# A two-layer gated cross-attention kernel: the order of its first DMAs and of its plane traffic is rewritten

## The chip, the cores and the metric

The kernel runs on one core of one Trainium2 chip. The metric is the device time of one execution in microseconds (us); lower is better.

## The reference

Two layers of gated cross-attention work on x of 4 x 512 rows of 256 numbers, with a context of the same size. The change touches the first layer's attention and what is prepared ahead of it:

```python
K = heads(ctx @ Wk.T + bk); V = heads(ctx @ Wv.T + bv)      # 16 heads of 16
Q = heads(layernorm(x) @ Wq.T + bq)
scores = Q @ K.T / 4 - 0.1 * abs(t_k - t_q)                  # 512 x 512 per head and batch
x = x + tanh(g_xattn[0]) * (softmax(scores) @ V @ Wo.T + bo)
x = x + tanh(g_ffn[0]) * (relu(layernorm(x) @ Wq1.T + b1) @ Wq2.T + b2)   # weights rounded to -1, 0, 1
# the second layer: the same attention with relu and no bias, then a layer with 4 experts
```

## The kernel before

Five engines each run a program of their own, written out by hand and tied together by semaphores: TensorE (PE), VectorE (DVE), ScalarE (ACT), GpSimd (POOL), and SyncE (SP), which issues most DMAs. An engine runs its program strictly in order, so a wait holds all that stands behind it.

**The prologue** (0 to 71.9 us) makes K, V and Q of the four batches b = 0 to 3. For each batch PE projects the keys (`project(0, "k", b, c)`, two halves c), the values (`values`), turns the normalised rows (`turn_n0`) and projects the queries. ACT and DVE bring each result out of PSUM in two parts, high and low, into `planes`. This buffer has four units: keys of a batch in units 0 and 1, queries in 2 and 3. So ACT may write the keys of batch b + 1 (`unit_out`) only when SP has stored those of batch b to HBM and the store has landed (`planes_kept0_i`). SP's `store_planes` stores planes with four DMAs each, and `load_stacks(g)` brings a group of four heads back with eight DMAs, laid out for the attention as `stack_q` and `stack_k`. There are 16 groups, four to a batch, and a ring of four stacks (`RING`): slots 0 to 3 are filled in the prologue, all of them from the planes of batch 0.

ACT issues the inputs of the batches 1 to 3 (`load_inputs`) and, after batch 2, seven late loads (`load_rest`). POOL splits the context into parts and copies the rows of constants (`constant_rows`, for the time bias) into all eight half-slots of the stacks.

**The attention** of a group needs each query's maximum first. PE multiplies "raws" (`for_maximum`, eight pairs of heads and query tiles to a group), DVE reduces each pair to maxima, POOL splits them in two parts, PE turns them, ACT keeps them (`keep_maximum`), and SP sends them into the stack (`send_maximum(g)`, two DMAs). Only then may PE start the scores of group g: its first score waits for `max_sent0`. Raws run 14 pairs ahead (`AHEAD`). `FIRST_RAWS` says after which step of the prologue the first pairs stand: (0, 2) means two pairs from pair 0. After the prologue's last load of stacks SP does this, in this order:

```python
                planes_left(sp, l, 2 * B * C)
...
                    for s_ in "kvq":
                        sp.dma_start(w_qkv[s_][:], part(a[f"L1_W{s_}"])).then_inc(sem("w_layer1"), 16)
...
                for g in range(G):
                    if g + 1 < G:
                        send_maximum(g + 1)
```

Of the kernel before, what the change touches and what calls it, by code (L numbers as in the profile page):

```python
# [16 lines left out]
P = 128  # L17
# [24 lines left out]
FIRST_RAWS = {(2, "q", 0): (0, 2), (2, "q", 1): (2, 2),  # L42
              (3, "k", 0): (4, 2), (3, "k", 1): (6, 1), (3, "v", 0): (7, 1), (3, "v", 1): (8, 2),
# [80 lines left out]
def gated_blocks_program(nc, a, out):  # L124
    with ExitStack() as ctx:
# [243 lines left out]
        N_KEYS, N_VALUES, N_ROWS, N_IN, N_REST, N_ATT = 4, 3, 2, 2, 7, 4  # L369
# [72 lines left out]

        def rows_in(b):
            return x[:, b * QT:(b + 1) * QT, :], a["x"][b * S:(b + 1) * S, :].rearrange("(t p) d -> p t d", p=P)
# [22 lines left out]
        def _(sp):  # L467
            for signal, moves in (
                (loaded_keys, ((w_qkv["k"][:], part(a["L0_Wk"])), context_in(0), (bias_qk[:, 0, :], a["L0_bq"]),
                               (bias_qk[:, 1, :], a["L0_bk"]))),  # L470
                (loaded_rows, (rows_in(0), (ident[:], a["ident"]))),
                (loaded_values, ((w_qkv["v"][:], part(a["L0_Wv"])), (bias_v[:], a["L0_bv"].partition_broadcast(P)),
                                 (w_qkv["q"][:], part(a["L0_Wq"])))),
            ):
                for dst, src in moves:
                    sp.dma_start(dst, src).then_inc(signal, 16)
# [20 lines left out]
            for l in range(2):  # L497
# [30 lines left out]
                if l == 0:  # L528
                    store_planes("k", 0)
                    store_planes("q", 0)  # L530
                    planes_left(sp, 0, C)
                    load_stacks(0, "k")
                    store_planes("k", 1)
                    planes_left(sp, 0, 2 * C)
                    load_stacks(0, "q")
                    store_planes("q", 1)
                    load_stacks(1, "k")
                    store_planes("k", 2)
                    load_stacks(1, "q")
# [5 lines left out]
                    load_stacks(RING - 1)  # L545
                else:
# [40 lines left out]
                if l == 0:  # L587
                    clear_rows(G)
                    sp.wait_ge(sem("normalised0"), G)
                    sp.dma_start(w1_raw[:], part(a["L0_W1"])).then_inc(sem("w_ffn0"), 16)  # L590
                    sp.dma_start(w2_raw[:], part(a["L0_W2"])).then_inc(sem("w_ffn0"), 16)
# [5 lines left out]
        def _(pe):  # L597
# [7 lines left out]
            def project(l, s_, b, c, src):  # L605
# [12 lines left out]
                else:  # L618
                    weights, rows = weight_parts(l, s_), src(b)
                    for i, (r, w) in enumerate(PRODUCTS):  # L620
# [5 lines left out]
                        if i == 0 and (l, s_, b) == (0, "q", 0):  # L626
                            pe.wait_ge(sem("parts_low"), C + 5)
# [11 lines left out]
            def values(l, v):  # L639
# [3 lines left out]
                if v == 0 and l == 0:  # L643
                    pe.wait_ge(sem("parts_low"), C + 4)
# [153 lines left out]
            def attention(l):  # L798
# [31 lines left out]
                def scores(g, k, t):  # L830

                    if k == 0 and t == 0:
                        pe.wait_ge(sem(f"max_sent{l}_{g % 2}"), 32 * (g // 2 + 1))
# [1322 lines left out]
```

## Time and profile before

| | before |
|---|---|
| three runs | 740.12 us median (739.31 to 741.78) |
| profiled execution | 741.31 us, span 739.5 us |
| PE busy | 691.2 us (93%) |
| DVE busy | 567.0 us (77%) |
| ACT busy | 453.1 us (61%) |
| POOL busy | 368.8 us (50%) |

The span is what the trace shows of the profiled execution; 1.8 us of its own time lie around it. Busy shares are averages over stages with different limits, so the rows further down are of single stretches.

### The profile page before, as it was taken

The page shows a single profiled execution, that of the slowest core. Times are in us where ns is not written, and L with a number is a line of the kernel's source. Part 1 is how long each engine was busy: PE and PEld are TensorE (multiplying, and loading weights), DVE is VectorE, ACT ScalarE, POOL GpSimd, SP SyncE. Part 2 cuts the span into 40 slices and gives each one's busy share as a digit, 9 for nine tenths or more (in the row PEclk, how much of TensorE's full clock was granted, in tenths as well). Part 3 has the DMA queues.
Part 4 walks back from the last instruction along what each step waited for, and adds up shares of the span by engine and source line. Part 5 has one row for each costly group of instructions (what it writes and reads, how often), then busy time and mean ns, then how long its engine had stood idle before and what let it go on. Part 6 is the DMA issues. An engine that isn't in the chain of part 4 may idle for free.

```text
span 739.5 us, 12829 instructions
## 1 busy us (share of the span) xinstructions
PE 691.2 (93%) x4390; PEld 434.9 (59%) x4390; DVE 567.0 (77%) x1037; ACT 453.1 (61%) x972; POOL 368.8 (50%) x442
## 2 busy tenths in 40 slices
PE   7886999999999899999999999999999899999993
PEld 5654444444443588788663444444444688999983
DVE  6786899999993267575888999999997667666673
ACT  3413888888888464856316888888887324333330
POOL 4641566565555433864500022645662756665543
PEclk9998999999999999999999999999999999999998
DMA  5898645555545434003134455432201432211100
GB/s 184 273 252 220 204 148 178 185 152 181 178 168 217 137 97 132 26 1 101 43 104 121 124 156 180 130 97 78 78 2 60 120 127 73 66 38 44 34 9 16
DMA packets 51423, 87.56 MB, mean 118 GB/s; under 512 B 8661, under 2 KB 16855, under 8 KB 51360
## 3 DMA queue, kind: packets, MB, share of 16 engines
q1 hardware_dynamic: 43184, 71.39, 31.1%
q0 software_dynamic: 4640, 11.54, 5.6%
q10 hardware_dynamic: 3536, 3.81, 2.0%
q8 instruction: 36, 0.59, 0.3%
q14 instruction: 27, 0.22, 0.1%
HBM read 44.92 MB, written 41.63 MB: 117 GB/s over the span
## 4 chain that ended last, share of the span: by engine, by line
PE 59%; POOL 10%; issue 9%; DVE 8%; SPq 5%; DMA 5%; ACT 2%; POOLq 0%; another core or an unknown queue 0%; DVEq 0%; ACTq 0%
PE ps_out L856 10%; PE ps_wide L1053 6%; PE ps_out L1076 6%; PE ps_wide L725 6%; PE ps_a L839 6%; SPq L517 3%; PE ps_a L978 3%; PE ps_misc L839 3%; POOL w_lo L1377 3%; PE ps_a L635 2%; PE ps_a L1065 2%; DMA stack_q<-planes_q 2%; PE ps_out L992 2%; PE ps_wide L652 2%; PE ps_misc L992 1%
## 5 line engine op out<-in xcount | busy, mean ns | idle before, releaser
L1688 DVE TENSOR_REDUCE row_max<-ps_wide 128x2 f32<-128x1024 f32 x256 | 301.7, 1220 | 21.1 <-PE ps_wide L725 20.3
L1199 ACT ACTIVATE probs<-ps_a 128x512 f32<-128x512 f32 (+1 forms) x418 | 199.1, 522 | 28.6 <-PE ps_a L839 26.7
L725 PE MATMUL ps_wide<-stack_k,stack_q 48*128 48x512 f32 x512 | 145.1, 470 | 11.6 <-DVE row_max L1688 4.3
L839 PE MATMUL ps_a<-stack_q,stack_k 62*128 62x512 f32 (+3 forms) x418 | 137.3, 391 | 2.1 <-ACT probs L1199 1.5
L856 PE MATMUL ps_out<-probs,vals 128*17 128x512 f32 x1024 | 134.1, 598 | 0.5 <-POOL probs L1455 0.5
L1199 ACT ACTIVATE probs<-ps_misc 128x512 f32<-128x512 f32 (+1 forms) x222 | 114.0, 514 | 16.5 <-PE ps_misc L839 13.8
L1455 POOL TENSOR_TENSOR probs<-probs,fixes_sb 128x512 f32<-128x512 f32 x64 | 82.2, 1284 | 79.1 <-ACT probs L1199 79.1
L839 PEld LDWEIGHTS ps_a<-stack_q,stack_k 62*128 62x128 f32 (+1 forms) x418 | 63.5, 184 | 67.4 <-ACT probs L1199 30.9
L725 PEld LDWEIGHTS ps_wide<-stack_k,stack_q 48*128 48x128 f32 x512 | 68.4, 184 | 47.0 <-DVE row_max L1688 26.2
L839 PE MATMUL ps_misc<-stack_q,stack_k 62*128 62x512 f32 (+3 forms) x222 | 87.8, 396 | 1.3 <-ACT probs L1199 1.2
L839 PEld LDWEIGHTS ps_misc<-stack_q,stack_k 62*128 62x128 f32 (+1 forms) x222 | 40.9, 184 | 39.1 <-ACT probs L1199 30.4
L1341 ACT ACTIVATE hid1T_hi<-ps_a 128x512 fp32r<-128x512 f32 x38 | 20.8, 598 | 49.6 <-PE ps_a L1065 49.6
L1440 POOL TENSOR_SCALAR max_neg<-row_max 128x16 f32<-128x16 f32 x32 | 8.1, 253 | 85.2 <-DVE row_max L1688 85.0
L1332 ACT ACTIVATE hid<-ps_wide 128x512 f32<-128x512 f32 x38 | 22.7, 599 | 37.2 <-PE ps_wide L1055 37.2
L1076 PE MATMUL ps_out<-w_mo_hi,hid1T_hi 128*128 128x256 f32 x152 | 44.3, 292 | 0.2 <-DVE sorted_rows L2042 0.2
L1076 PE MATMUL ps_out<-w_mo_hi,hid1T_lo 128*128 128x256 f32 x152 | 42.7, 281 | 0.0
L1076 PE MATMUL ps_out<-w_mo_lo,hid1T_hi 128*128 128x256 f32 x152 | 42.7, 281 | 0.0
L1522 POOL TENSOR_TENSOR hid_lo<-hid_full,hid_hi 128x512 fp32r<-128x512 f32 x24 | 30.8, 1303 | 20.3 <-ACT hid_hi L1295 20.3
L1358 POOL TENSOR_TENSOR root<-var_eps,minus_half 128x4 f32<-128x4 f32 x16 | 17.6, 1097 | 43.1 <-DVE var_eps L1634 42.9
L856 PEld LDWEIGHTS ps_out<-probs,vals 128*17 128x17 f32 x1024 | 17.5, 95 | 33.1 <-issue 15.7
L1431 POOL TENSOR_TENSOR planes<-full,planes 128x512 fp32r<-128x512 f32 x16 | 21.6, 1361 | 29.5 <-ACT planes L1137 26.1
L1294 ACT ACTIVATE hid_full<-ps_a,b_cols 128x512 f32<-128x512 f32 x32 | 22.1, 692 | 19.3 <-PE ps_a L978 15.7
(288 smaller groups left out, 1413.1 us busy)
## 6 DMA issues: line engine op xcount, KB each, us to landing
rows_sorted<-blank SPq DMA_DIRECT2D x17, 1040.0 KB, 5.0
planes_k<-planes SPq DMA_DIRECT2D x32, 256.0 KB, 3.7
planes_q<-planes SPq DMA_DIRECT2D x32, 256.0 KB, 3.8
stack_k<-planes_k SPq DMA_DIRECT2D x64, 128.0 KB, 2.9
stack_q<-planes_q SPq DMA_DIRECT2D x64, 128.0 KB, 2.8
w_raw<-in_L_W SPq DMA_DIRECT2D x6, 1024.0 KB, 5.3
stack_k<-planes_k SPq DMA_DIRECT2D x64, 64.0 KB, 2.6
stack_q<-planes_q SPq DMA_DIRECT2D x64, 64.0 KB, 2.7
```

What stands on the lines that cost most here:

```text
L517: sp.dma_start(stack[rows, slot(g):slot(g) + 2 * S].bitcast(F32).rearrange("r (c t) -> r c t", t=S), src[:, i]).then_inc(sem(f"stack_loade ...
L725: mm(raw_slot(l, ("pair", g, p))[:, i * S:(i + 1) * S], stack_q[at, slot(g, c) + q * P:slot(g, c) + (q + 1) * P], stack_k[at, slot(g, c):s ...
L839: mm(score_slot(("tile", n))[:, start:end], stack_k[at, slot(g, c) + k * P:slot(g, c) + (k + 1) * P], stack_q[at, slot(g, c) + start:slot( ...
L856: mm(po[32 * j:32 * j + VW, :], vals[:, k, g * HG + j, :], probs[n % PROBS[l]][:, j, :], start=(k == 0), stop=(k == QT - 1)).then_inc(sem( ...
L992: last = mm((po, pm)[t % 2][:, 0:D], hidden0(b, rows, f)[:, q * P:(q + 1) * P], w2_q[:, f, :], start=(f == 0 and h == 0), stop=(f == FC - ...
L1053: mm(bank, sortedT[r][:, n % 2, c, :], w1_flat[w][:, bass.ds(at + (c * FF + half * S), S)], start=(i == 0 and c == 0), stop=False)
L1076: last = mm(po[:, 0:D], hid1T[r][:, n % 2, f, :], w_mo_part(w, f), start=(f == 0 and i == 0), stop=(f == FC - 1 and i == 2))
L1199: do(probs[n % PROBS[l]][:, j, start:end], score_slot(("tile", n * TILES + t))[:, start:end], ACT.Exp, scale=0.25).then_inc(exp_done, 1)
L1332: do(hid1[:, n % 2, half * S:(half + 1) * S], pw[0][:, half * S:(half + 1) * S], ACT.Gelu).then_inc(sem("hid1_ready"), 1)
L1455: v.tensor_tensor(block_, block_, fixes[:, k % 2, :].unsqueeze(1).broadcast_to([P, HG, P]), ALU.mult).then_inc(sem("fixed"), 1)
L1522: v.tensor_tensor(hidden0(b, "lo", f), hid0_full[:, u % 4, :], hidden0(b, "hi", f), ALU.subtract).then_inc(sem("hid0_low"), 1)
L1688: v.tensor_reduce(row_max[:, g % 2, :, p], raw_slot(l, ("pair", g, p))[:].rearrange("p (i k) -> p i k", i=2), AX, ALU.max).then_inc(sem(f" ...
```

## The change

1. SP's nine first loads come in another order, each with a semaphore as its users need it: the key weight, the context, the value weight, the rows, the identity, the query weight, and the three biases last. The high part of the value weight is made by ACT instead of DVE. ACT starts the inputs of batch 1 behind these parts instead of ahead of them.
2. SP waits for all planes of batch 0, loads the whole stack of group 0 and only then stores the planes of batch 1; the stack of group 1 stands whole between the planes of batches 1 and 2.
3. Two pairs of raws move ahead, into the values of batch 2; of the later ones one each stands in the keys and values of batch 3.
4. Of the seven late loads on ACT's queue three stay. The other four (`w_o`, `bias_2`, `b1_cols`, `order`) go to SP's queue, behind the weights of the second layer.
5. POOL copies the constant rows into the half-slots 1 to 3 only. SP copies the half-slots 0 to 3 to 4 to 7 (four DMAs) behind the last load of stacks; PE waits for them ahead of group 2.

```diff
-FIRST_RAWS = {(2, "q", 0): (0, 2), (2, "q", 1): (2, 2),
-              (3, "k", 0): (4, 2), (3, "k", 1): (6, 1), (3, "v", 0): (7, 1), (3, "v", 1): (8, 2),
+FIRST_RAWS = {(2, "v", 0): (0, 1), (2, "v", 1): (1, 1), (2, "q", 0): (2, 2), (2, "q", 1): (4, 2),
+              (3, "k", 0): (6, 1), (3, "k", 1): (7, 1), (3, "v", 0): (8, 1), (3, "v", 1): (9, 1),
               (3, "q", 0): (10, 2), (3, "q", 1): (12, 2)}
...
                     store_planes("k", 0)
                     store_planes("q", 0)
-                    planes_left(sp, 0, C)
-                    load_stacks(0, "k")
+                    planes_left(sp, 0, 2 * C)
+                    load_stacks(0)
                     store_planes("k", 1)
-                    planes_left(sp, 0, 2 * C)
-                    load_stacks(0, "q")
                     store_planes("q", 1)
-                    load_stacks(1, "k")
+                    load_stacks(1)
                     store_planes("k", 2)
-                    load_stacks(1, "q")
                     store_planes("q", 2)
                     load_stacks(RING - 2)
                     store_planes("k", 3)
                     send_maximum(0)
                     store_planes("q", 3)
                     load_stacks(RING - 1)
+                    sp.wait_ge(sem("rows_in0"), 16 * 2 * N_ATT)
+                    sp.wait_ge(loaded_rest, 16 * (N_FIRST + N_REST))
+                    for i in range(2):
+                        for rows in constant_rows(i):
+                            sp.dma_start(rows[:, RING * S:].bitcast(F32), rows[:, 0:RING * S].bitcast(F32)).then_inc(loaded_rest, 16)
...
                     for s_ in "kvq":
-                        sp.dma_start(w_qkv[s_][:], part(a[f"L1_W{s_}"])).then_inc(sem("w_layer1"), 16)
+                        sp.dma_start(w_qkv[s_][:], part(a[f"L1_W{s_}"])).then_inc(loaded_context, 16)
+                    for dst, src in ((w_o[:], part(a["L0_Wo"])), (bias_2[:], a["L0_b2"].partition_broadcast(P)),
+                                     (b1_cols[:], a["L0_b1"]), (order[:], a["order"])):
+                        sp.dma_start(dst, src).then_inc(loaded_context, 16)
...
+            act.wait_ge(loaded_values, 16)
+            do(w_v_hi0[:], w_qkv["v"][:], ACT.Copy).then_inc(sem("parts_high"), 1)
+            load_inputs(1)
+            act.wait_ge(loaded_rest, 16 * N_FIRST)
...
                 for dst, src in (
-                    (w_o[:], part(a["L0_Wo"])), (gates_raw[:], a["gates"].partition_broadcast(P)),
-                    (bias_o[:], a["L0_bo"].partition_broadcast(P)), (bias_2[:], a["L0_b2"].partition_broadcast(P)),
-                    (b1_cols[:], a["L0_b1"]), (fixes[:], a["fixes"]), (order[:], a["order"]),
+                    (gates_raw[:], a["gates"].partition_broadcast(P)), (fixes[:], a["fixes"]),
+                    (bias_o[:], a["L0_bo"].partition_broadcast(P)),
                 ):
...
-                            pool.dma_start(rows[:, S:].rearrange("r (n t) -> r n t", t=S),
-                                           rows[:, 0:S].unsqueeze(1).broadcast_to([n, RING * 2 - 1, S])).then_inc(sem("rows_in0"), 16)
+                            pool.dma_start(rows[:, S:RING * S].rearrange("r (n t) -> r n t", t=S),
+                                           rows[:, 0:S].unsqueeze(1).broadcast_to([n, RING - 1, S])).then_inc(sem("rows_in0"), 16)
```

SP's program between the planes of batch 0 and those of batch 2, in the kernel before (`planes_k` and `planes_q` are the stores, `stack_k` and `stack_q` the loads; x4 and x2 count DMAs):

```order
L506 DMA planes_q<-planes 64x2x512 x4
L517 DMA stack_k<-planes_k 16x2x512 x2
L517 DMA stack_k<-planes_k 32x2x512 x2
L506 DMA planes_k<-planes 64x2x512 x4
L517 DMA stack_q<-planes_q 32x2x512 x2
L517 DMA stack_q<-planes_q 16x2x512 x2
L506 DMA planes_q<-planes 64x2x512 x4
```

The same place in the changed kernel:

```order
L514 DMA planes_q<-planes 64x2x512 x4
L525 DMA stack_q<-planes_q 32x2x512 x2
L525 DMA stack_q<-planes_q 16x2x512 x2
L525 DMA stack_k<-planes_k 16x2x512 x2
L525 DMA stack_k<-planes_k 32x2x512 x2
L514 DMA planes_k<-planes 64x2x512 x4
L514 DMA planes_q<-planes 64x2x512 x4
```

The key planes of batch 1 are stored behind eight loads where they were behind four, and those loads wait for the query planes of batch 0.

SP's program from the last load of stacks to the maxima of group 1 (`max_rows`), in the kernel before:

```order
L517 DMA stack_k<-planes_k 32x2x512 x2
L567 DMA w_k<-in_L_Wk 128x2x256
L567 DMA w_v<-in_L_Wv 128x2x256
L567 DMA w_q<-in_L_Wq 128x2x256
L524 DMA stack_q<-max_rows 2x8x128 x2
```

And in the changed kernel:

```order
L525 DMA stack_k<-planes_k 32x2x512 x2
L555 DMA stack_q<-stack_q 12x2048
L555 DMA stack_k<-stack_k 14x2048
L555 DMA stack_q<-stack_q 12x2048
L555 DMA stack_k<-stack_k 14x2048
L577 DMA w_k<-in_L_Wk 128x2x256
L577 DMA w_v<-in_L_Wv 128x2x256
L577 DMA w_q<-in_L_Wq 128x2x256
L580 DMA w_o<-in_L_Wo 128x2x256
L580 DMA bias<-in_L_b 128x256
L580 DMA b_cols<-in_L_b 128x8
L580 DMA order_sb<-in_order 128x4
L532 DMA stack_q<-max_rows 2x8x128 x2
```

Eight DMAs more stand ahead of the maxima of group 1.

## Rows read from the trace of the kernel before

**Rows 1.** The chain that ended last, 0 to 92 us: start, us, what.

```profile
48.44 12.22 DMA stack_q<-planes_q
...
81.42 2.38 DMA stack_q<-max_rows
...
83.84 0.38 PE ps_a L839
```

**Rows 2.** Windows: stretch, us, busy of PE, PEld, DVE, ACT, POOL, clock, DMA, GB/s.

```profile
41.90:56.80 14.90, 12.40 (x63) 7.93 (x61) 14.59 (x27) 2.08 (x4) 7.13 (x9) 1.00 1.22 209
56.80:60.70 3.90, 0.04 (x1) 0.00 (x0) 0.69 (x1) 1.72 (x3) 3.11 (x5) 0.95 1.11 296
60.70:67.20 6.50, 6.02 (x19) 4.02 (x19) 4.10 (x5) 1.34 (x3) 0.06 (x1) 0.50 0.79 231
67.20:71.90 4.70, 3.40 (x15) 1.74 (x15) 3.77 (x5) 1.47 (x3) 0.00 (x0) 1.00 0.68 194
83.80:94.60 10.80, 10.76 (x71) 4.60 (x71) 9.34 (x9) 9.10 (x22) 7.31 (x9) 1.00 0.53 175
```

**Rows 3.** Timeline of ACT, 22 to 60 us: start, us, instruction, idle before.

```profile
34.86 0.69 ACT L1136 ACTIVATE full<-ps_a,bias_qk 128x512 f32<-128x512 f32 x1 [1.25 <-PE ps_a L635]
...
40.54 0.60 ACT L1162 ACTIVATE x_hi<-ps_misc 128x512 fp32r<-128x512 f32 x1 [0.41 <-PE ps_misc L908]
...
56.10 0.69 ACT L1136 ACTIVATE full<-ps_a,bias_qk 128x512 f32<-128x512 f32 x1 [10.29 <-issue]
```

**Rows 4.** Timeline of SP's DMA issues, 20 to 67 us.

```profile
28.27 3.29 SPq L506 DMA_DIRECT2D planes_k<-planes  x4
31.73 2.92 SPq L517 DMA_DIRECT2D stack_q<-planes_q  x4
34.69 3.90 SPq L506 DMA_DIRECT2D planes_q<-planes  x4
...
44.82 6.55 SPq L517 DMA_DIRECT2D stack_q<-planes_q  x4
51.41 6.00 SPq L506 DMA_DIRECT2D planes_q<-planes  x4
```

**Rows 5.** Issued in 23.9 to 25.2 and 34.6 to 38.6 us: KB each, median us to landing.

```profile
planes_q<-planes SPq DMA_DIRECT2D x1, 256.0 KB, 5.4
...
planes_q<-planes SPq DMA_DIRECT2D x4, 256.0 KB, 6.2
```

**Rows 6.** Timeline of DVE, 5 to 73 us.

```profile
11.06 0.43 DVE L1921 CAST w_v_hi<-w_v 128x512 fp32r<-128x512 f32 x1 [0.40 <-DMA w_q<-in_L_Wq]
...
41.17 0.69 DVE L1908 TENSOR_TENSOR x_lo<-ps_misc,x_hi 128x512 fp32r<-128x512 f32 x1 [0.31 <-ACT x_hi L1162]
...
61.58 2.36 DVE L1688 TENSOR_REDUCE row_max<-ps_wide 128x2 f32<-128x1024 f32 x2 [4.00 <-PE ps_wide L725]
...
68.14 0.75 DVE L1662 SCALAR_TENSOR_TENSOR planes<-ps_a,bias_qk,planes 128x512 fp32r<-128x512 f32 x1 [2.28 <-ACT planes L1137]
```

**Rows 7.** Timeline of SP's DMA issues, 71 to 84 us.

```profile
71.83 1.23 SPq L506 DMA_DIRECT2D planes_q<-planes  x2
73.10 3.01 SPq L517 DMA_DIRECT2D stack_q<-planes_q  x4
76.16 2.85 SPq L517 DMA_DIRECT2D stack_k<-planes_k  x4
79.19 0.43 SPq L567 DMA_DIRECT2D w_k<-in_L_Wk  x1
...
80.69 1.36 SPq L524 DMA_DIRECT2D stack_q<-max_rows  x2
```

**Rows 8.** Timeline of PE, 65 to 86 us.

```profile
71.91 1.02 PE L603 MATMUL ps_out<-vals 128*17 128x512 f32 x2 [0.21 <-DVE planes L1662]
...
82.65 1.05 PE L856 MATMUL ps_out<-probs,vals 128*17 128x512 f32 x8
```

**Rows 9.** POOL's copies of the constant rows, issued in 45.6 to 48.1 us.

```profile
stack_k<-stack_k POOLq DMA_DIRECT2D x2, 196.0 KB, 10.3
stack_q<-stack_q POOLq DMA_DIRECT2D x2, 168.0 KB, 8.9
```

More of the change, by code:

```diff
@@ L368, in gated_blocks_program @@
         loaded_rest = sem("loaded_rest")
[L369 removed]
+        loaded_context, loaded_queries = sem("context0_then_layer1"), sem("queries0_then_ffn0")
+        N_FIRST, N_IN, N_REST, N_ATT = 4, 2, 3, 4
         block = ctx.enter_context(nc.Block())
@@ L467, in _ @@
         def _(sp):
[L468 to L473, printed above, removed]
-            ):
-                for dst, src in moves:
-                    sp.dma_start(dst, src).then_inc(signal, 16)
+            for signal, dst, src in (
+                (loaded_keys, w_qkv["k"][:], part(a["L0_Wk"])),
+                (loaded_context, *context_in(0)),
+                (loaded_values, w_qkv["v"][:], part(a["L0_Wv"])),
+                (loaded_rows, *rows_in(0)),
+                (loaded_rest, ident[:], a["ident"]),
+                (loaded_queries, w_qkv["q"][:], part(a["L0_Wq"])),
+                (loaded_rest, bias_qk[:, 0, :], a["L0_bq"]),
+                (loaded_rest, bias_qk[:, 1, :], a["L0_bk"]),
+                (loaded_rest, bias_v[:], a["L0_bv"].partition_broadcast(P)),
+            ):
+                sp.dma_start(dst, src).then_inc(signal, 16)
             def load_last(n):
@@ L589, in _ @@
                     sp.wait_ge(sem("normalised0"), G)
-                    sp.dma_start(w1_raw[:], part(a["L0_W1"])).then_inc(sem("w_ffn0"), 16)
-                    sp.dma_start(w2_raw[:], part(a["L0_W2"])).then_inc(sem("w_ffn0"), 16)
+                    sp.dma_start(w1_raw[:], part(a["L0_W1"])).then_inc(loaded_queries, 16)
+                    sp.dma_start(w2_raw[:], part(a["L0_W2"])).then_inc(loaded_queries, 16)
             for i in range(LANDING):
@@ L902, in turn_n0 @@
             def turn_n0(b):
+                if b == 0:
+                    pe.wait_ge(loaded_rest, 16 * N_FIRST)
                 pe.wait_ge(sem("normed"), QT * (b + 1))
@@ L1917, in _ @@
                                 ).then_inc(sem("parts_low"), 1)
-            dve.wait_ge(loaded_rows, 16 * N_ROWS)
+            dve.wait_ge(sem("parts_high"), C + 1)
+            weight_low("v")
+            dve.wait_ge(loaded_rows, 16)
             variance(0, 0, x, 1e-5)
-            dve.wait_ge(loaded_values, 16 * N_VALUES)
-            v.tensor_copy(w_v_hi0[:], w_qkv["v"][:]).then_inc(sem("parts_low"), 1)
-            dve.wait_ge(sem("parts_low"), C + 3)
-            weight_low("v")
             normal(0, 0, x)
-            dve.wait_ge(sem("parts_high"), C + 1)
+            dve.wait_ge(sem("parts_high"), C + 2)
             weight_low("q")
+            dve.wait_ge(loaded_rest, 16 * N_FIRST)
             for b in range(B):
```

34 lines of the change are left out of this document (16 added, 18 removed).

## The prediction

> **What bounds the kernel now.** I read the chain that ended last first. Up to 92 us it shows two waits that are no engine's work: the load of group 1's query stack takes 12.22 us, from 48.44 to 60.67, and PE starts behind it [rows 1]; and the maxima of group 1, sent by SP at 81.42, land 2.38 us later, just when PE takes the scores of group 1 at 83.84 [rows 1]. The windows come next. From 83.8 us PE is busy for 10.76 of 10.8 us [rows 2]: in the attention PE is the bound, one group takes about 10.8 us, and time lost there is not won back. In the prologue it is another matter. DVE is full from 41.9 to 56.8 (14.59 of 14.9 us). Then PE stands still for 3.9 us, and behind this wait the granted clock is 0.50 from 60.7 to 67.2, which is 1.2 GHz instead of 2.4 [rows 2]. In these two stretches and up to 71.9 DVE has only 0.69 + 4.10 + 3.77 = 8.56 us of work in 15.1.
>
> The queues say why. ACT stood for 10.29 us in front of the keys of batch 3, with "issue" as the reason, since it was issuing the seven late loads [rows 3], and SP needed 6.55 us for four loads and 6.00 for four stores, which took 2.92 and 3.29 earlier [rows 4]. All of this falls together with POOL's copies of the constant rows, which landed 8.9 and 10.3 us after their issue [rows 9]. So the prologue has something to give. The rest of the argument is what the new order takes.
>
> **The start of the attention.** I call the moment when PE starts it T0; it is 71.9 now [rows 8]. What I need is the new T0.
>
> First loads: DVE waited 0.40 us at 11.06 for the query weight before it could split the value weight [rows 6]. This goes, and the context's parts begin earlier; but ACT now waits for the biases, which are issued last, ahead of its first results. Below, the gain is nothing if the biases land as late as the query weight did (11.0); above, it is 1.2 us, the time by which the value projection could begin earlier. I take 0.6.
>
> Plane traffic: the last query plane of batch 0 was issued at 23.9 and landed 5.4 us later, at 29.3 [rows 5]; with the 0.6 at 28.7. Until then SP now stands still, where it used to load and store. Eight loads at 0.63 to 0.73 us (2.92 for four [rows 4]) take it to about 33.8. The key planes of batch 1, which were issued at 28.27 [rows 4], are now issued from 33.8 to 37.7, in the place and at the price of the four stores at 34.69 (3.90 us [rows 4], landing after 6.2 us [rows 5], because the inputs of batch 3 are on their way then). So the first half lands at about 41.1 (issued 34.9) and the second at about 43.2. ACT may not write the keys of batch 2 before that: its instruction at 34.86 [rows 3] moves to 41.1. Behind it in ACT's program stand the other half and the two copies of the turned rows: 41.1 + 1.3 = 42.4, the second half from 43.2 to 44.5, two copies of 0.60 to 45.7. The second copy ended at 41.1 before [rows 3]. Batch 2 is thus 4.6 us late, and DVE's last low part of it ends at 46.5 instead of 41.9 [rows 6]. If the stores land after 3.9 us or so, this is 2.3 us less.
>
> From there DVE sets the pace. From 41.9 to 71.9 it was busy for 14.59 + 0.69 + 4.10 + 3.77 = 23.2 us [rows 2]. Two of its reductions now stand ahead of this point, at 2.36 us for two [rows 6]: 20.8 remain. The wait of 4.00 us for the stack [rows 6] goes, since group 1's stack is loaded before POOL's copies begin, which are also 3 of 7 parts of what they were. ACT's seven issues become three. The last wait, 2.28 us [rows 6], lay at the half clock; I keep 1.1 of it and 0.6 for small ones. New T0: 46.5 + 20.8 + 1.7 = 69.0, which is **2.9 us earlier**. Bounds: nothing, if PE's own wait in batch 2 (about 3.5 us between the turned rows and the queries) lets the clock fall there too; and 9 us, if batch 2 is not held at all, from 15.1 - 8.56 = 6.5 of idle DVE and 2.4 of moved reductions.
>
> **The maxima of group 1.** They hang on SP's queue, counted from T0, because SP's last stores wait for the same result of DVE as PE does (71.83 against 71.91 [rows 7, 8]). Before: the stores from 71.83, eight loads of stacks, three weights, and the maxima issued at 80.69 [rows 7], landed 2.38 us after the second of them, at 83.8 [rows 1], which is T0 + 11.9. PE was through with what it could do at 83.7 (82.65 + 1.05 [rows 8]), T0 + 11.8: no slack at all. Now eight DMAs stand in between. The four copies of constants, at the 0.63 us and the gap of a stack load: 4 x 0.64 = 2.6 us. The four loads from HBM, at the 0.43 us and gap of a weight (three took from 79.19 to 80.69 [rows 7]): 4 x 0.49 = 2.0. The maxima then land at T0 + 16.5 and PE waits 4.7 us. Behind the waiting score stand all of PE's raws and weighted sums, so DVE and ACT run dry too.
>
> The landing can also be late: the copies of constants and 1.2 MB of weights and biases lie ahead in the same queue. By POOL's rows, 728 KB took about 10 us [rows 9], 416 KB in four copies would take 6 to 8 us from T0 + 7.4, the weights behind them 3 more, and the maxima would land up to 2 us later. Below it is nothing. SP's other transfers were faster than POOL's, so I add 0.5: **5.2 us of wait**. The Trainium skill ("DMA: Bandwidth & Descriptors", section on the anatomy of one DMA) gives a DMA 2.0 us plus its bytes at 436 GB/s. By that, an estimate, a copy of 112 KB is done in 2.3 us, the addition is nothing and the wait 4.7; POOL's rows, with 8.9 and 10.3 us, do not agree with the page.
>
> **The clock.** A PE wait of 3.9 us was followed by 6.5 us at 0.50 [rows 2]. The new wait is longer, so the clock falls again, now in the stretch where PE is the bound. At its end the old wait had barely reached the fall (mean 0.95 [rows 2]); the new one takes 1.2 us or so of the slow stretch into itself. The 5.4 us left at half speed cost **2.7 us**. Bounds: 0 and 3.3.
>
> **What costs nothing.** The four late loads are used only behind the attention, some 170 us later. PE's new wait ahead of group 2 is for copies that landed a group earlier. The split of the value weight on ACT (0.6 us) lies in ACT's idle start; without that cover it would cost its 0.6.
>
> **The sum.** -2.9 + 5.2 + 2.7 = +5.0 us. Against the profiled execution (741.31 us, span 739.5) that is 746.3; its time is 1.2 us above the median of the runs, 740.12, so for the median I say **745.1 us**.
>
> **Rivals.**
> 1. The start wins nothing: the held batch 2 brings a PE wait with the half clock behind it. For: the 3.9 us wait did so. Against: DVE is busy there and hides some of it. +5.2 + 2.7 and 1.5 for slow projections: +9.4, 749.5 us. Chance 0.18.
> 2. The start wins most of DVE's idle time, 6.5 us, because the stores land soon and ACT is hardly held. +1.4, 741.5 us: no difference. For: other stores land in 4 us when no inputs are on their way. Against: the place of the stores at 34.69 [rows 4, 5]. Chance 0.15. That the change does not do what it says, the maxima being as early as before, would end here too; the order of SP's program excludes it.
> 3. Faster: the prologue loses all its waits and the two moved reductions are free. T0 comes 9 us earlier, and the wait for the maxima stays at 4.7 without a fall of the clock. -4.3, 735.8 us. It decides from 7.9 us of gain at T0 with the fall, from 4.7 without it. For: DVE's idle time adds up to it. Against: SP is idle until 28.7 with 34 us of issues to do, and a wait above 3.9 us without a fall was not seen. Chance 0.07.
> My forecast has 0.60, and its own range is 743 to 748. The range reaches to the cases 1 and 2: 741.0 to 750.0; outside lie rival 3 and the edges of 1 and 2, under 2 in 10. A change under 0.3% (2.2 us) can't be told from none here. Slower 0.77 (the forecast without its lowest edge, and rival 1), same 0.15, faster 0.08.
>
> **What would show it.** Right: T0 near 69 in PE's timeline; ACT's first instruction for the keys of batch 2 near 41, released by a store; no load of stacks over 8 us; SP's maxima of group 1 issued 12.7 us or more behind its last plane stores; a PE wait of 4.5 to 6 us ahead of the first scores of group 1, and a window of half clock behind it. Wrong: that wait is missing or short, or T0 is below 64; or a wait for the second copies of constants stands in front of group 2.

## The result and the profile after

| | before | after |
|---|---|---|
| four runs each | 740.32 us median (739.31 to 741.78) | 748.72 us median (747.47 to 750.60) |
| ratio | | 1.011, 95% interval 1.009 to 1.0131 |
| profiled execution | 741.31 us, span 739.5 us | 747.47 us, span 745.7 us |
| PE busy | 691.2 us | 698.0 us |
| start of the attention (T0) | 71.91 | 70.73 |
| first scores of group 1 | 83.84 | 88.98 |
| first scores of group 1, counted from T0 | 11.93 | 18.25 |

The change makes the kernel 1.1% slower (8.4 us, from 740.32 to 748.72). The start comes 1.18 us sooner and the first scores of group 1 come 5.14 us later. By the end of group 1 the distance is 6.2 us, at 400 us it still is, and so is the distance of the two spans: what comes behind group 1 adds nothing on balance.

ACT's timeline of the changed kernel, 0 to 60 us (start, us, instruction, idle before), answers to [rows 3]:

```profile
11.27 0.69 ACT L1151 ACTIVATE full<-ps_a,bias_qk 128x512 f32<-128x512 f32 x1 [3.13 <-DMA bias_v<-in_L_bv]
...
43.30 0.69 ACT L1151 ACTIVATE full<-ps_a,bias_qk 128x512 f32<-128x512 f32 x1 [8.02 <-DMA planes_k<-planes]
...
46.33 0.61 ACT L1177 ACTIVATE x_hi<-ps_misc 128x512 fp32r<-128x512 f32 x1
...
57.41 0.69 ACT L1151 ACTIVATE full<-ps_a,bias_qk 128x512 f32<-128x512 f32 x1 [3.94 <-issue]
```

The second row is the held batch 2. ACT stands for 8.02 us, and the releaser is the store that SP now issues behind eight loads. The last row is the gain of part 4, 3.94 us of issuing instead of 10.29. The first row is new: ACT waits 3.13 us for the biases, and its first result comes at 11.27.

SP's DMA issues, 29 to 88 us, answer to [rows 4, 7]:

```profile
29.75 2.53 SPq L525 DMA_DIRECT2D stack_q<-planes_q  x4
32.33 2.50 SPq L525 DMA_DIRECT2D stack_k<-planes_k  x4
34.87 3.16 SPq L514 DMA_DIRECT2D planes_k<-planes  x4
...
51.46 5.66 SPq L514 DMA_DIRECT2D planes_q<-planes  x4
57.16 3.65 SPq L525 DMA_DIRECT2D stack_q<-planes_q  x4
...
78.31 0.89 SPq L555 DMA_DIRECT2D stack_q<-stack_q  x1
79.25 0.81 SPq L555 DMA_DIRECT2D stack_k<-stack_k  x1
80.10 0.72 SPq L555 DMA_DIRECT2D stack_q<-stack_q  x1
80.86 0.76 SPq L555 DMA_DIRECT2D stack_k<-stack_k  x1
81.80 0.43 SPq L577 DMA_DIRECT2D w_k<-in_L_Wk  x1
82.27 1.26 SPq L577 DMA_DIRECT2D w_v<-in_L_Wv  x1
83.57 0.47 SPq L577 DMA_DIRECT2D w_q<-in_L_Wq  x1
84.09 0.47 SPq L580 DMA_DIRECT2D w_o<-in_L_Wo  x1
...
86.06 1.38 SPq L532 DMA_DIRECT2D stack_q<-max_rows  x2
```

From the first copy to the maxima 7.75 us pass, where the three weights before took 1.50 [rows 7]: 6.25 us for the eight DMAs more. The four copies take 3.49 of them (0.72 to 0.89 each), the four late loads 1.97, and the weights take 2.29 instead of 1.50. The stores of batch 1 (34.87) landed 7.3 us after their issue (median of the four):

```profile
planes_k<-planes SPq DMA_DIRECT2D x4, 256.0 KB, 7.3
```

PE's timeline, 10 to 92 us, answers to [rows 8]:

```profile
15.98 0.63 PE L926 MATMUL ps_out<-ident_sb,rows_all 128*128 128x128 f32 x4 [2.93 <-DVE vals L1680]
...
46.99 1.22 PE L648 MATMUL ps_a<-x_hi,w_q_hi 128*128 128x512 f32 x2 [4.24 <-ACT x_hi L1177]
...
70.73 1.02 PE L616 MATMUL ps_out<-vals 128*17 128x512 f32 x2 [0.21 <-DVE planes L1675]
...
83.51 1.05 PE L871 MATMUL ps_out<-probs,vals 128*17 128x512 f32 x8
88.98 0.58 PE L854 MATMUL ps_a<-stack_q,stack_k 62*128 62x256 f32 x1 [4.41 <-DMA stack_q<-max_rows]
```

And the windows at these places, with the columns of [rows 2]:

```profile
17.10:23.90 6.80, 6.11 (x15) 4.80 (x15) 3.91 (x12) 1.91 (x4) 5.38 (x6) 0.50 0.87 245
44.40:51.20 6.80, 4.21 (x11) 2.52 (x12) 3.78 (x12) 3.09 (x6) 6.26 (x7) 0.50 0.93 293
51.20:70.70 19.50, 16.90 (x83) 10.71 (x83) 18.33 (x27) 5.93 (x11) 6.60 (x10) 1.00 0.85 207
...
84.60:88.80 4.20, 0.00 (x0) 0.00 (x0) 0.48 (x1) 0.00 (x0) 2.87 (x3) 1.00 0.88 249
88.80:92.20 3.40, 3.22 (x17) 1.64 (x17) 1.97 (x2) 2.34 (x5) 0.00 (x0) 0.50 0.42 121
```

The reader is to see three waits of PE (2.93, 4.24 and 4.41 us), each with a stretch at 0.50, that is 1.2 GHz, at its end or shortly behind. Between 51.2 and 70.7 us DVE sets the pace, with 18.33 of 19.5 us. From 84.6 to 88.8 PE and ACT stand still, DVE has 0.48 us and POOL 2.87 us of work: they wait for two small DMAs. A fourth stretch of half clock falls into group 0:

```profile
70.70:84.60 13.90, 13.83 (x59) 5.49 (x59) 11.15 (x10) 9.26 (x21) 4.52 (x7) 0.75 0.72 170
```

The same 59 matmuls took 11.8 us before, from 71.9 to 83.7 [rows 8]; here PE is through at T0 + 13.8. These 2.0 us hide a part of the wait. So the maxima landed 6.3 us later from T0, and only 4.4 of that shows as a wait.

### The profile page after: what moved, and what is told of

It is laid out like the page before. It is cut to its first block, busy times and chain, and to the rows that moved or that the text cites. A ratio compares the mean times of both kernels' runs of the same rounds, so it can differ in the third digit from the quotient of the medians.

```text
span 745.7 us, 12834 instructions
## 1 busy us (share of the span) xinstructions
PE 698.0 (94%) x4390; PEld 438.7 (59%) x4390; DVE 565.7 (76%) x1036; ACT 454.0 (61%) x973; POOL 369.0 (49%) x442
## 4 chain that ended last, share of the span: by engine, by line
PE 60%; POOL 10%; DVE 9%; issue 9%; SPq 5%; DMA 4%; ACT 3%; POOLq 0%; DVEq 0%; ACTq 0%
PE ps_out L871 10%; PE ps_wide L1068 7%; PE ps_out L1091 6%; PE ps_wide L738 6%; PE ps_a L854 6%; PE ps_a L993 3%; PE ps_a L648 3%; PE ps_misc L854 3%; POOL w_lo L1394 3%; SPq L525 3%; PE ps_a L1080 2%; DVE row_max L1701 2%; PE ps_out L1007 2%; PE ps_wide L665 2%; PE ps_misc L1007 1%
## 5 line engine op out<-in xcount | busy, mean ns | idle before, releaser
L1214 ACT ACTIVATE probs<-ps_a 128x512 f32<-128x512 f32 (+1 forms) x418 | 199.2, 522 | 34.6 <-PE ps_a L854 34.1
L738 PE MATMUL ps_wide<-stack_k,stack_q 48*128 48x512 f32 x512 | 147.0, 476 | 5.3 <-DVE row_max L1701 2.0
L1214 ACT ACTIVATE probs<-ps_misc 128x512 f32<-128x512 f32 (+1 forms) x222 | 114.0, 514 | 18.1 <-PE ps_misc L854 15.2
L854 PEld LDWEIGHTS ps_a<-stack_q,stack_k 62*128 62x128 f32 (+1 forms) x418 | 64.3, 188 | 71.9 <-ACT probs L1214 31.3
L854 PE MATMUL ps_misc<-stack_q,stack_k 62*128 62x512 f32 (+3 forms) x222 | 88.8, 400 | 1.3 <-ACT probs L1214 1.2
L1358 ACT ACTIVATE hid1T_hi<-ps_a 128x512 fp32r<-128x512 f32 x38 | 20.8, 598 | 47.8 <-PE ps_a L1080 47.8
```

The lines of the kernel that those rows point to most:

```text
L738: mm(raw_slot(l, ("pair", g, p))[:, i * S:(i + 1) * S], stack_q[at, slot(g, c) + q * P:slot(g, c) + (q + 1) * P], stack_k[at, slot(g, c):s ...
L854: mm(score_slot(("tile", n))[:, start:end], stack_k[at, slot(g, c) + k * P:slot(g, c) + (k + 1) * P], stack_q[at, slot(g, c) + start:slot( ...
L1214: do(probs[n % PROBS[l]][:, j, start:end], score_slot(("tile", n * TILES + t))[:, start:end], ACT.Exp, scale=0.25).then_inc(exp_done, 1)
```

## The experiments

Each was timed beside the kernel before on the same chip; ratios are to it, with 95% intervals. The kernel before had a median of 739.81 us beside e1 to e4, 742.04 beside e5 to e8, 740.84 beside e9 to e11 and 740.50 beside e12, so times of different groups are compared by their ratios. A trace is of one execution. My theory after the result: (a) SP's queue ahead of the maxima costs about 6 us; (b) the new order of the plane traffic holds batch 2 and costs part of what the rest wins at the start; (c) the waits bring the half clock, which costs too. The rivals: the start alone is to blame, or the clock is.

### e1: the maxima of group 1 ahead of the copies

```diff
                     load_stacks(RING - 1)
+                    send_maximum(1)
...
-                    if g + 1 < G:
+                    if g + 1 < G and (l, g) != (0, 0):
                         send_maximum(g + 1)
```

> The changed kernel, but SP sends the maxima of group 1 right behind the last load of stacks, ahead of the copies of constants, the weights and the four late loads. My theory (the issues of SP's queue): the maxima land near 11 to 12 us behind the start of the attention, PE's wait of 4.4 us ahead of the scores of group 1 and the half clock behind it are gone, and the time falls by 5 to 6 us, to about 743. Rival (the landing is late because of the bytes in the queues, or PE has another wait at this place): a wait of 2 us or more stays, and the time is 746 or more.

Measured: 746.41 us (745.44 to 750.21), ratio 1.0097 (1.0067 to 1.0127). The wait at group 1 was gone and stood at group 2; of the 5 to 6 us that I expected about one came (1.0097 against 1.011, with intervals that overlap), and the time is the rival's. SP's issues in this kernel, 76 to 98 us, then PE's timeline at 99 us:

```profile
79.09 1.33 SPq L532 DMA_DIRECT2D stack_q<-max_rows  x2
80.55 0.84 SPq L556 DMA_DIRECT2D stack_q<-stack_q  x1
...
89.07 2.55 SPq L525 DMA_DIRECT2D stack_q<-planes_q  x4
91.66 2.50 SPq L525 DMA_DIRECT2D stack_k<-planes_k  x4
94.20 0.58 SPq L502 DMA_DIRECT2D rows_sorted<-blank  x1
94.83 1.95 SPq L532 DMA_DIRECT2D stack_q<-max_rows  x2
```

```profile
99.49 0.58 PE L855 MATMUL ps_a<-stack_q,stack_k 62*128 62x256 f32 x1 [4.93 <-DMA stack_q<-max_rows]
```

From 80.55 SP issues without a pause up to the next maxima, 14.3 us later, where a group lasts 10.8. The queue was not shortened, so the wait moved on by one group. Moving one urgent transfer ahead is not enough when the rest still fills more than a group's time.

### e2 and e3: the old order of the plane traffic, and that with e1's edit

```diff
-                    planes_left(sp, 0, 2 * C)
-                    load_stacks(0)
+                    planes_left(sp, 0, C)
+                    load_stacks(0, "k")
                     store_planes("k", 1)
+                    planes_left(sp, 0, 2 * C)
+                    load_stacks(0, "q")
                     store_planes("q", 1)
```

and so on, with group 1's stack in two parts and `FIRST_RAWS` as before.

> The changed kernel with the old order of SP's loads and stores in the prologue and the old places of the raws. My theory (the held batch): ACT's wait of 8.0 us for the store of the keys of batch 1, PE's 4.2 us and the half clock from 44.4 to 51.2 are gone, the attention starts 3 to 5 us earlier (at 66 to 68), and the wait for the maxima of group 1 stays: about 744.5. Rival (DVE sets the pace anyway, and the old order brings its own late stack): the attention starts within 1.5 us of 70.7 and the time is 747 or more.

> Both edits of the two runs ahead of this one. My theory: the two losses add up, 748.7 - 5.5 - 4.2 = 739, about the kernel before or 1 us faster. Rival (they overlap, since an earlier attention finds SP later): only one of the two gains is seen, 743 to 744.

Measured: e2 746.80 us (744.89 to 747.95), ratio 1.0089 (1.0063 to 1.0114); e3 745.89 us (741.69 to 747.23), 1.0077 (1.0051 to 1.0104). The hold of batch 2 is gone in e2 (ACT's keys come at 36.73 with 1.25 us of waiting for PE, and PE waits 0.69 us for the turned rows where it waited 4.24), but T0 is 69.02 and not the 66 to 68 that I expected. The wait for the maxima of group 1 stays, 3.98 us, and in e3 it stands at group 2 with 4.95. So undoing the order does not make the kernel fast; the wait for the maxima stands there with either order. Both times miss the theory, e2's by 2 us and e3's by 7; e3's lies over its rival's 743 to 744 as well, because the wait had only moved on, as in e1.

### e4: parts 4 and 5 alone on the kernel before, with the early maxima

```diff
                     load_stacks(RING - 1)
+                    send_maximum(1)
+                    sp.wait_ge(sem("rows_in0"), 16 * 2 * N_ATT)
+                    sp.wait_ge(loaded_rest, 16 * N_REST)
+                    for i in range(2):
+                        for rows in constant_rows(i):
+                            sp.dma_start(rows[:, RING * S:].bitcast(F32), rows[:, 0:RING * S].bitcast(F32)).then_inc(loaded_rest, 16)
```

and the four late loads behind the weights, POOL's copies for the half-slots 1 to 3.

> The kernel before with only the late loads and the split copies of constants of the change, and the maxima of group 1 sent right behind the last load of stacks: so e3 without the new first loads. My theory (the first loads cost the changed kernel about 1.5 us, by PE's wait of 2.9 us at 13 and the half clock behind it): 1 to 2 us under e3, about 737.5. Rival (the new first loads are worth the 0.6 us that I predicted): about 0.6 us over e3.

Measured: 744.42 us (741.97 to 747.33), ratio 1.0074 (1.0047 to 1.0101). T0 is 67.19, the earliest of all, 4.7 us ahead of before; then PE waits 4.99 us at group 2 with 6.8 us at the half clock behind it. The expected 737.5 us are missed by 7: in this trace the start gains 4.7 us, and the queue takes more than all of it.

### e5 and e6: nothing bulky ahead of the maxima

On the changed kernel (e5), and on the kernel before with parts 4 and 5 (e6), e1's edit and:

```diff
-                    for s_ in "kvq":
-                        sp.dma_start(w_qkv[s_][:], part(a[f"L1_W{s_}"])).then_inc(loaded_context, 16)
-                    for dst, src in ((w_o[:], part(a["L0_Wo"])), (bias_2[:], a["L0_b2"].partition_broadcast(P)),
...
                         send_maximum(g + 1)
+                    if l == 0 and g == 2:
+                        for s_ in "kvq":
+                            sp.dma_start(w_qkv[s_][:], part(a[f"L1_W{s_}"])).then_inc(loaded_context, 16)
+                        for dst, src in ((w_o[:], part(a["L0_Wo"])), (bias_2[:], a["L0_b2"].partition_broadcast(P)),
...
```

> The changed kernel, but SP sends the maxima of group 1 right behind the last load of stacks, copies the constants then, and issues the three weights and the four late loads only in group 2, behind the maxima of group 3. The run with the maxima first alone moved the wait of PE to group 2 (4.9 us). My theory (eight issues and three more don't fit into SP's queue ahead of the maxima of groups 1 and 2): no PE wait over 1 us in the attention, and the time is that of the changed kernel without its wait and the half clocks of the attention, 748.7 - 7 = about 741.5. Rival (what counts are the bytes of the copies, or the order only moves the wait on to group 3): a wait of 3 us or more at one of the groups 1 to 4, and 745 or more.

> The kernel before with only the late loads and the split copies of the change, in the spread form of the run ahead. My theory: the attention starts at about 67.2 as in the earlier run of this base, with no wait in it, so 4 to 5 us under the kernel before: 735 to 736. Rival (the early start is lost to a wait, or the clock): within 1.5 us of the kernel before.

Measured: e5 742.59 us (741.55 to 747.3), ratio 1.0022 (1.0005 to 1.004); e6 740.40 us (737.91 to 743.22), ratio 0.9978 (0.996 to 0.9996). In e5 the longest wait of the attention is 1.28 us, at group 2. Compared with the changed kernel (1.011) that is 0.9% or 6.5 us: theory (a), with the half clock behind the wait in it. What e5 still loses against e6, 0.44% or 3 us, goes with parts 1 to 3. The time of e6 was expected 4 to 5 us below the kernel before and is 1.6 below it (740.40 against 742.04), near the rival's 1.5: its T0 is 69.59 where e4 with the same prologue had 67.19, and a wait of 0.88 us is left at group 2.

### e7: PE kept at work in the wait

On the changed kernel, four matmuls of zeros ahead of the first scores of group 1 (the trace counts two instructions for each):

```diff
+                    if (l, g, k, t) == (0, 1, 0, 0):
+                        score_free(("tile", QT * TILES))
+                        keep_going(score_slot(("tile", QT * TILES))[:], blank[:, 0:P], blank[:, 0:S], 4)
```

> The changed kernel with four matmuls of zeros on PE (about 4.1 us) in the wait for the maxima of group 1. My theory (the wait lets the clock fall and costs more than itself): the wait ends as before, the half clock behind it is gone, and the time falls by 1.5 to 3 us, to about 746.5. Rival (the clock costs nothing there): no difference, 748 to 749.

Measured: 750.44 us (748.04 to 752.38), ratio 1.0118 (1.0092 to 1.0144): none of the 1.5 to 3 us that I expected. PE's timeline, 84 to 94 us, and a window:

```profile
84.18 3.70 PE L616 MATMUL ps_a<-blank 128*128 128x512 f32 x8
90.15 0.38 PE L857 MATMUL ps_a<-stack_q,stack_k 62*128 62x256 f32 x1 [2.27 <-DMA stack_q<-max_rows]
```

```profile
91.80:95.20 3.40, 3.40 (x17) 1.52 (x16) 1.90 (x3) 1.94 (x5) 1.92 (x4) 0.50 0.45 136
```

PE was busy for 3.70 us and idle for 2.27, and the clock fell all the same, for 3.4 us from 91.8, as long as in the changed kernel. In this execution the maxima were also issued 1.3 us later, at 87.4. A fill for the whole wait wasn't tried, so whether one would keep the clock is open; this part of a fill won nothing.

### e8: parts 2 and 3 alone on the kernel before

```diff
-                    planes_left(sp, 0, C)
-                    load_stacks(0, "k")
-                    store_planes("k", 1)
                     planes_left(sp, 0, 2 * C)
-                    load_stacks(0, "q")
+                    load_stacks(0)
+                    store_planes("k", 1)
                     store_planes("q", 1)
-                    load_stacks(1, "k")
+                    load_stacks(1)
                     store_planes("k", 2)
-                    load_stacks(1, "q")
                     store_planes("q", 2)
```

and the new `FIRST_RAWS`; nothing else.

> The kernel before with only the new order of SP's loads and stores in the prologue and the sooner raws. My theory (the held batch): ACT waits 6 to 8 us for the first store of the keys of batch 1, PE 3 to 4 us in batch 2; with the late loads and the seven copies still in the prologue, the attention starts at or behind 72: 740 to 743. Rival (the order is good in itself, since it brings group 1's stack in time): the attention starts at 69 or earlier, 737.

Measured: 748.74 us (746.85 to 750.59), ratio 1.0091 (1.0065 to 1.0116), and T0 at 78.75, 6.8 us later than before. ACT's timeline with its DMA issues, and SP's issues:

```profile
43.59 0.69 ACT L1133 ACTIVATE full<-ps_a,bias_qk 128x512 f32<-128x512 f32 x1 [8.83 <-DMA planes_k<-planes]
...
53.50 5.60 ACTq L1235 DMA_DIRECT2D gates_raw<-in_gates  x1
59.13 3.72 ACTq L1235 DMA_DIRECT2D bias_o<-in_L_bo  x1
...
66.38 0.69 ACT L1133 ACTIVATE full<-ps_a,bias_qk 128x512 f32<-128x512 f32 x1 [12.61 <-issue]
```

```profile
52.44 11.16 SPq L506 DMA_DIRECT2D planes_q<-planes  x4
```

One issue of a small load took 5.60 us of ACT's time. ACT's seven late loads begin at 53.1 instead of 45.1 as before, 8.0 us later, and its wait behind them is 12.61 us instead of 10.29; so the keys of batch 3 come 10.3 us later, and ACT's issues are the longest piece of the chain. They ran beside POOL's copies before too (issued from 45.6 there, from 51.2 here), so what made them slower by 2.3 us is not shown. My expectation had the order cost too little: it counted the hold and not the late loads behind it. It did not have a PE wait of 3.31 us for group 0's key stack at 42.25 either, which e9 shows in full.

### e9: the changed kernel with the old first loads

Part 1 undone, with all its semaphores:

```diff
+            for signal, moves in (
+                (loaded_keys, ((w_qkv["k"][:], part(a["L0_Wk"])), context_in(0), (bias_qk[:, 0, :], a["L0_bq"]),
+                               (bias_qk[:, 1, :], a["L0_bk"]))),
...
+            load_inputs(1)
...
-            do(w_v_hi0[:], w_qkv["v"][:], ACT.Copy).then_inc(sem("parts_high"), 1)
-            load_inputs(1)
```

> The changed kernel with part 1 undone: the nine first loads in their old order with their old semaphores, the value weight's high part on DVE again, ACT's inputs of batch 1 issued ahead of its parts. Theory: the new first loads cost about 1.5 us instead of winning 0.6, since the three biases land last and ACT's first keys wait for them. Then ACT writes its first keys at about 9.7 us instead of 11.3, there is no PE wait of 2.9 us at 13 us and no stretch of half clock before 25 us, the start of the attention comes 1.0 to 1.7 us earlier (69.0 to 69.7), the wait for the maxima of group 1 stays at 4.2 to 4.6 us, and the time is 1 to 2.5 us below the changed kernel, 746 to 747.5. Rival: DVE, which is full from 47 us on, hides what the start does; then the start of the attention stays at 70.5 to 71 and the time at 748 to 749.

Measured: 750.11 us (749.25 to 750.42), ratio 1.0124 (1.0106 to 1.0142). ACT's first keys come at 10.63 instead of 11.27, the wait at 13 us is 0.86 and no half clock follows it. Yet T0 is 71.89 and the time no better than that of the changed kernel, whose interval it overlaps. The theory, that part 1 costs time, falls. The rival was that DVE hides what the start does. The early start is indeed lost, but T0 and the time lie 1 us over the rival's numbers, and the chain goes through another wait, which neither theory nor rival had. It lies in batch 2, and the half clock runs from 40.7 to 47.5:

```profile
41.44 0.79 PE L734 MATMUL ps_wide<-stack_k,stack_q 48*128 48x512 f32 x2 [3.60 <-DMA stack_k<-planes_k]
```

Part 3 has put the first raws into the values of batch 2, and they read group 0's stacks. Here the last of the loads was issued at 34.4 and landed 7.0 us later, PE stood for it, and the values and turned rows behind it came late: DVE's last low part of the batch ends at 49.0, in the changed kernel at 47.8. In the changed kernel's trace the same raws, at 39.19, wait for nothing; in e1, e5 and e7 they wait 1.3 to 1.7 us. PE's timeline in this kernel shows the wait without the help of a slow group 0 (there is no half clock from 47.5 to 88.5 us):

```profile
90.12 0.58 PE L850 MATMUL ps_a<-stack_q,stack_k 62*128 62x256 f32 x1 [6.42 <-DMA stack_q<-max_rows]
```

### e10, e11 and e12: parts 4 and 5 as they are, the early maxima alone, part 4 alone

e10 is e4 without `send_maximum(1)`. e11 is the kernel before with e1's edit and nothing else. e12 is e6 without part 5: POOL copies all constant rows as before.

```diff
                 for dst, src in (
-                    (w_o[:], part(a["L0_Wo"])), (gates_raw[:], a["gates"].partition_broadcast(P)),
...
-                    if g + 1 < G:
+                    if g + 1 < G and (l, g) != (0, 0):
                         send_maximum(g + 1)
+                    if l == 0 and g == 2:
+                        for s_ in "kvq":
+                            sp.dma_start(w_qkv[s_][:], part(a[f"L1_W{s_}"])).then_inc(sem("w_layer1"), 16)
...
```

> The kernel before with parts 4 and 5 alone, as the change has them: three late loads stay on ACT's queue, four go behind the weights of the second layer on SP's, and SP copies half of the constant rows behind the last load of stacks. Theory: start of the attention at 67 to 70 us (the copies and late loads no longer collide with the stacks of group 1), maxima of group 1 at 12.7 us or more behind the last plane stores, a PE wait of 4 to 5 us there and then 1 to 2 us for half clock: 742 to 745 us, slower than before by 0.2 to 0.7%. Rival 1, that SP's queue costs nothing when the order of the plane traffic is the old one: 737 to 739. Rival 2, that the wait costs 5 and the start wins nothing: 747 or more.

> The kernel before with one edit: the two DMAs with the maxima of group 1 stand directly behind the last load of stacks, ahead of the three weights. In the kernel before these maxima landed just when PE was through. Theory of the queue: each DMA ahead of them counts only where PE waits; here the wait is about zero, so that the edit wins nothing: 739 to 741.5, same. The maxima of group 2 keep their place with no wait at them. Rival: in most executions PE does wait a little at group 1, since there was no slack; then 0.5 to 1.5 us are won.

> The kernel before with part 4 alone, and nothing of it ahead of the early maxima: POOL copies all the constant rows as before; the maxima of group 1 stand directly behind the last load of stacks; the three weights and the four late loads stand in the loop of group 2, behind the maxima of group 3. Theory (the gain of the best version comes from the copies of part 5, which collide with the stacks of group 1): the load of group 1's stack still takes 10 us or more, the start of the attention stays at 70 to 72 us, no PE wait over 1 us at groups 1 to 3, and the time is 738.5 to 740.5, no different from before. Rival (ACT's seven late issues are what held the prologue): ACT's issue wait falls from 10.3 to about 5 us, the start comes at 68 to 69.5, and the time is 736.5 to 738.5, below the best version so far.

Measured: e10 745.97 us (743.55 to 747.42), ratio 1.006 (1.004 to 1.008); e11 740.65 us (739.32 to 742.79), 0.9996 (0.998 to 1.0012); e12 739.10 us (737.55 to 742.36), 0.9981 (0.9962 to 1.0). PE's timeline of e10:

```profile
67.97 1.02 PE L615 MATMUL ps_out<-vals 128*17 128x512 f32 x2 [0.21 <-DVE planes L1671]
...
85.96 0.58 PE L853 MATMUL ps_a<-stack_q,stack_k 62*128 62x256 f32 x1 [6.20 <-DMA stack_q<-max_rows]
```

e10 shows the whole trade by itself: 3.9 us won at the start, 6.20 lost in the wait, more lost to the clock. I had expected a wait of 4 to 5 us as in the changed kernel, where group 0 ran partly at the half clock and hid the rest; the time is 1 us over the expected range. e11 says that the early maxima are worth nothing where PE does not wait for them. e12 splits the gain at the start. I had put it down to part 5, and that falls: the start is the rival's, though the time is still the theory's. With the copies on POOL as before, T0 is 68.44 and ACT has no issue wait left at the keys of batch 3 (its late loads are done at 48.0, and it then waits 3.86 us for PE). So the number of ACT's late loads is what held the prologue, as far as one trace shows it: e11, with the prologue of before, has a T0 of 70.70. SP is still held in e12, 8.29 us for four stores, and nobody waits for it:

```profile
49.20 8.29 SPq L510 DMA_DIRECT2D planes_q<-planes  x4
```

Of its 3.5 us at T0, 1.7 arrive at the end of the span: a stretch of half clock, 6.8 us from 69.5, now lies in group 0, where PE is the bound.

### The maxima of group 1 in six kernels

All times from the traces, in us; the last three columns count from T0.

| kernel | T0 | maxima issued | PE through | scores of group 1 | wait |
|---|---|---|---|---|---|
| before | 71.91 | +8.8 | +11.8 | +11.9 | 0.1 |
| after | 70.73 | +15.3 | +13.8 | +18.3 | 4.41 |
| e2 | 69.02 | +15.2 | +13.9 | +17.9 | 3.98 |
| e9 | 71.89 | +15.1 | +11.8 | +18.2 | 6.42 |
| e10 | 67.97 | +15.2 | +11.8 | +18.0 | 6.20 |
| e11 | 70.70 | +7.1 | +11.7 | +11.7 | 0 |

In all four kernels with eight DMAs more ahead of them, whatever their prologue, these scores come 6.0 to 6.3 us later from T0. Where group 0 ran partly at the half clock, PE only arrives later and waits less.

## Why the prediction was right, and where it was off

The sign, the places and the chain of causes were right, but the size was short: 5.0 us slower were forecast and 8.4 measured. The median of 748.72 lies 3.6 above the predicted 745.1, inside the whole range (741.0 to 750.0) but outside the 743 to 748 that the forecast called its own; it got there by part of rival 1. The steps one by one:

1. **The held batch 2.** Right in kind and nearly in size. ACT's keys of batch 2 were foreseen at 41.1, released by a store, and came at 43.30, released by a store. The stores were issued at 34.87 instead of 33.8 and landed in 7.3 us instead of 6.2. DVE's last low part of the batch ended at 47.8 instead of 46.5, as its timeline shows (start and length):

```profile
47.09 0.68 DVE L1921 TENSOR_TENSOR x_lo<-ps_misc,x_hi 128x512 fp32r<-128x512 f32 x1
```

2. **The start of the attention, mis-sized.** The step "T0 69.0, 2.9 us earlier" measured 70.73, or 1.2 earlier; 1.3 of the missing 1.7 us are step 1's. The term in it for the first loads (0.6 won) is nothing here: the query planes of batch 0 landed at 29.7 instead of 28.7, and in e9, with the old first loads, at 29.8. ACT's first result even moved from 9.7 to 11.3 us, since it now waits for the last of nine loads, the biases, where the first group of four used to do. Single traces set a bound to what can be said of T0: e4, e6 and e10 have the same prologue and show 67.19, 69.59 and 67.97; after, e1, e5 and e7 share one too and show 70.2 to 71.9; e2 and e3, with the new first loads and the old order, show 69.0 and 69.9. Before and e11 share one as well and show 71.9 and 70.7. So parts 2 and 3 cost 0.4 to 2.9 us at T0 with the new first loads and 2.3 to 4.7 with the old ones (e9), and parts 4 and 5 win 1.1 to 4.7. The prediction had a gain of 2.9 in all; the trace has 1.2, and executions of one prologue differ by up to 2.4. The raws moved by part 3 were taken as free; that they can stand for group 0's stack (3.60 us in e9, 1.3 to 1.7 in e1, e5 and e7) was not foreseen.
3. **The PE wait in batch 2 with the half clock behind it** was rival 1's mechanism. It came (4.24 us, then 0.50 from 44.4 to 51.2), and DVE hid a part of it, as the text against this rival said. The start still won 1.2 us in this trace, so that the outcome lies between forecast and rival 1 (749.5), and the median lies nearer to the rival.
4. **The maxima of group 1.** Right in kind; the term was too small. I had 4.6 us for eight DMAs and 0.5 for a late landing, 5.1 together; e9 and e10 measured 6.3 and 6.1. That the wait itself (4.41) looks close to the 5.2 forecast is luck: it is short of the 4.5 to 6 that I gave as the sign, because an unforeseen half clock in group 0 hid 2.0 us of it; without that e9 and e10 have 6.42 and 6.20. The four loads from HBM cost what was said (1.97 for 2.0). The copies cost 3.49 instead of 2.6: a copy from SBUF to SBUF holds SP's queue for 0.72 to 0.89 us here, where I had taken a stack load's 0.63. The weights behind them took 0.8 more. The landing was not late at all, 2.15 us after the second maxima's issue. 
   The Trainium skill ("DMA: Bandwidth & Descriptors", the section on the anatomy of one DMA) gives 2.0 us plus the bytes at 436 GB/s, measured on GpSimd's path: an estimate of 2.0 us for 8 KB, with which these 2.15 us agree. The DMAs just ahead do not: the 256 KB weights landed after 3.9 to 4.5 us, where it gives 2.6 (an estimate), and `order` with 2 KB after 3.4. The estimate of a 4.7 us wait that went with it is short of the 6.4 and 6.2 of e9 and e10 as well, because the issue grew and not the landing.
5. **The clock.** "The 5.4 us left at half speed cost 2.7" took half of the stretch as lost. Counted from the first scores of group 1 to the end of the first attention, after loses 1.1 us on 3.2 us at 0.50, e9 1.7 on 5.2, e10 1.9 on 5.6 against the kernel before: about a third of the stretch, not a half. In return a second stretch, which I had not foreseen, lay in group 0 and cost 2.0 us on 6.8, and all of that was hidden by the wait.
6. **The sum** for the profiled execution: -1.2 + 2.0 + 4.3 + 1.1 = 6.2 us, against 5.0 forecast; 747.5 against 746.3.
7. **The step from the profiled execution to the median** failed by twice as much as the sum: I took off 1.2 us, since the profiled run before lay that far above its median. The changed kernel's profiled run is the fastest of its four, 1.25 us below the median. Together 2.4 of the 3.6 us. One trace of a kernel whose runs spread over 3 us does not carry a correction of this kind, and it should have gone into the range instead.

Nothing waited for the second copies of constants in front of group 2, and no load of stacks took over 8 us, as foreseen. The best versions are e12 and e6, with ratios of 0.9981 and 0.9978. Their intervals end at 1.0 and 0.9996, so e12 can't be told from before and e6 hardly, and they are the best of twelve tried; e12 needs only that four loads leave ACT's queue and that nothing bulky stands ahead of the maxima.

Open: why the half clock falls at other places from execution to execution, and so how much of a microsecond won in the prologue reaches the end. Parts 1, 3 and 5 weren't run alone. My theories missed the times of e3, e4 and e8 by 5.7 to 6.9 us, e1's by 3.4 and those of e2 and e6 by 2 to 3. What sets how late the loads of group 0's stack land (7.0 us in e9) is open as well.

## What to carry to other kernels

On a queue that runs in order, ask of every transfer that is moved which small and urgent one stands behind it, and count the issue time of all of them up to the next due time: here eight DMAs that nobody waited for made two small ones 6 us late, and the engine that is the bound stood. Moving the urgent one ahead helps only if what is left fits into the time up to the next one (14.3 us against a group's 10.8 in e1, and the wait just moved on). Bulk loads with a far due time belong behind the point where the queue has slack, and off an engine whose results others wait for.

## What was not expected of the hardware

- A copy of 12 or 14 rows of 2048 words from SBUF to SBUF held SP's queue for 0.72 to 0.90 us, a load of a 256 KB weight for 0.43 to 0.58, and the second weight behind the copies for 1.24 to 1.40 (after, e2, e9, e10 and e1).
- The issue of a DMA took far longer at some places than at others: 5.60 us for the gates on ACT in e8 against 0.35 in after, and 8.29 (e12) and 11.16 us (e8) for four stores on SP against 3.0 to 3.2 for most sets of four in after. POOL's copies were under way each time, but also at the 0.35 us in after, so what makes an issue long is not shown.
- A stretch at 0.50 lasted 3.4 or 6.8 us in nearly all cases (10.2 once, in e10, of which 4.6 in the wait), and the attention's work lost about a third of such a stretch, not half: 13.8 us instead of 11.8 for the same 59 matmuls with 6.8 us at 0.50.
- The clock fell behind waits of 2 to 3 us too (2.93 in after, 1.98 in e6), and in e7 though PE had been busy for 3.70 of the 6.0 us.
